# Attention and expert block on one core: four pieces of vector work and three pieces of matmul work stand at other places of the sequence loop

## The reference

```python
q, k, v = (einsum(layernorm(x), W) for W in (Wq, Wk, Wv))       # 16 heads of 64
sim = 50 * tanh((q @ k.T) / 8 / 50)                             # causal mask behind it
x = x + softmax(sim) @ v @ Wo.T
t = layernorm(x)
shared = gelu(t @ sw1 + sb1) @ sw2 + sb2
probs = softmax(t @ gate_w + gate_b); top 2 of 8 experts per token
y_e = gelu(t @ w1[e] + b1[e]) @ w2[e] + b2[e]
x = x + sum of the two chosen probs[e] * y_e + shared
```

## Time and profile before

| What | Value |
|---|---|
| median of 3 runs | 2253.5 us (2251.34 to 2255.41) |
| the profiled execution's own time | 2243.76 us |
| its span | 2242.0 us |
| TensorE busy | 1976.0 us, 88% |
| VectorE busy | 1557.3 us, 69% |
| ScalarE busy | 1420.5 us, 63% |
| GpSimd busy | 1021.2 us, 46% |
| mean granted TensorE clock | 0.955 of full speed |

### The profile page before, as it was taken

One profiled execution on the slowest core, in us unless ns is written; L12 is line 12 of the kernel. 1 busy time (PEld: TensorE's weight loads), 2 busy tenths in 40 slices (PEclk: granted clock), 3 DMA queues, 4 the chain that ended last, 5 costly groups with the idle time before them and its releaser, 6 DMA issues.

```text
span 2242.0 us, 39929 instructions
## 1 busy us (share of the span) xinstructions
PE 1976.0 (88%) x14653; PEld 1542.8 (69%) x14653; DVE 1557.3 (69%) x2803; ACT 1420.5 (63%) x2170; POOL 1021.2 (46%) x1195
## 2 busy tenths in 40 slices
PE   6799898989898988898989899898998975699898
PEld 4577666666666666666667667666666653699898
DVE  4578686767777776767677776777677686566565
ACT  6678576757676757676766766676666652344444
POOL 3445354544454444454535353445354551544344
PEclk9999999999999999999999999999999987799999
DMA  3000000100000000000101010101010102765564
GB/s 122 1 10 20 20 29 20 30 20 20 29 20 29 20 29 20 15 34 12 37 10 39 10 39 10 38 10 39 10 39 1 39 25 98 217 190 172 158 186 142
DMA packets 73665, 112.51 MB, mean 50 GB/s; under 512 B 9715, under 2 KB 52218, under 8 KB 73476
## 3 DMA queue, kind: packets, MB, share of 16 engines
q1 hardware_dynamic: 58468, 67.86, 10.7%
q0 software_dynamic: 15008, 42.10, 5.0%
HBM read 63.10 MB, written 48.65 MB: 50 GB/s over the span
## 4 chain that ended last, share of the span: by engine, by line
PE 53%; DVE 34%; ACT 9%; issue 3%; DMA 1%; POOL 0%; DVEq 0%; SPq 0%; POOLq 0%
PE bank_o L1238 8%; DVE norm L796 6%; PE ring L1196 6%; PE ring L1217 4%; DVE q_lo L785 4%; DVE kT L780 4%; PE ring L1144 3%; PE ring L1222 3%; PE ring L1150 3%; PE ring L1145 3%; PE ring L1203 3%; ACT prob L591 3%; ACT prob L585 2%; DVE oTl L810 2%; DVE oTh L808 2%
## 5 line engine op out<-in xcount | busy, mean ns | idle before, releaser
L508 POOL TENSOR_SCALAR_AFFINE_SELECT prob<-prob 128x256 f32<-128x256 f32 x512 | 221.3, 454 | 692.4 <-ACT prob L591 692.3
L585 ACT ACTIVATE prob<-ring 128x1024 f32<-128x1024 f32 (+1 forms) x384 | 328.2, 877 | 257.6 <-PE ring L1222 254.0
L780 DVE TENSOR_TENSOR kT<-ring,kT 64x512 fp32r<-64x512 f32 x256 | 176.3, 689 | 319.7 <-ACT kT L598 315.2
L1238 PE MATMUL bank_o<-prob,v 128*32 128x512 f32 (+3 forms) x4096 | 328.2, 464 | 77.0 <-DVE weighed L801 66.3
L520 POOL TENSOR_TENSOR key_sum<-prob 128x768 f32<-128x768 f32 x128 | 245.5, 1918 | 248.2 <-PE bank_d L1252 236.5
L591 ACT ACTIVATE prob<-prob 128x1024 f32<-128x1024 f32 (+1 forms) x384 | 344.0, 914 | 5.2
L1238 PEld LDWEIGHTS bank_o<-prob,v 128*32 128x32 f32 x4096 | 122.6, 115 | 253.9 <-issue 168.2
L1217 PE MATMUL ring<-qT,kT 128*128 128x256 f32 (+3 forms) x1024 | 245.2, 342 | 52.3 <-DVE row L933 11.8
L1217 PEld LDWEIGHTS ring<-qT,kT 128*128 128x128 f32 x1024 | 171.2, 194 | 131.4 <-issue 67.7
L796 DVE RECIPROCAL norm<-bank_d 128x512 f32<-128x512 f32 x64 | 214.9, 3357 | 46.1 <-PE bank_d L1252 44.3
L1222 PE MATMUL ring<-q_lo,kT 128*128 128x256 f32 (+3 forms) x1024 | 231.9, 328 | 0.0
(11 more groups left out here) (224 smaller groups left out, 4742.4 us busy)
## 6 DMA issues: line engine op xcount, KB each, us to landing
xin<-first SPq DMA_DIRECT2D x71, 257.0 KB, 3.1
xin<-second SPq DMA_DIRECT2D x71, 129.0 KB, 2.4
xin<-base SPq DMA_DIRECT2D x71, 128.0 KB, 2.4
x_next<-in_x SPq DMA_DIRECT2D x16, 512.0 KB, 4.8
x_res<-in_x SPq DMA_DIRECT2D x16, 512.0 KB, 4.3
raw_e<-in_w SPq DMA_DIRECT2D x4, 1024.0 KB, 6.7
first<-pad SPq DMA_DIRECT2D x9, 257.0 KB, 4.7
second<-pad SPq DMA_DIRECT2D x9, 129.0 KB, 7.4
```

What stands on the lines that cost most here:

```text
L508: last = nc.gpsimd.affine_select(out=diag, in_=diag, compare_op=ALU.is_ge, fill=0.0, base=0, pattern=[[0, 2], [1, P]], channel_multiplier=-1)
L585: nc.scalar.activation(probs[p % PROBS][u][:, :, :], slot[:, :, 0:UNIT_COLS[u]], ACT.Tanh, scale=SCALE / SOFTCLAMP).then_inc(act_emptied, 1)
L780: last = nc.vector.tensor_tensor(kT[head_rows[1 - h], h, :], slot[r, 1, :], kT[r, h, :].bitcast(F32), ALU.subtract)
L1238: last = pe.matmul(bank_o[h * QD:(h + 1) * QD, j * P:N], v[:, j, f:f + QD], probs[(2 * quad + h // 2) % PROBS][u][:, h % 2, at:at + N - j ...
```

## The change

The change moves code and removes or adds no arithmetic. For TensorE: in pair 4 `project_out(i, 0)` stands behind `project_qk`; the last two pieces of the projection of sequence `i - 1`, 6 and 7, both stand in pair 2, one right behind the scores and one behind `project_v`, so pair 3 has none; in pair 5 `hidden` stands behind `values`, in front of `turn_logits`. For VectorE: `place_tokens` stands in front of `empty_qk` in pair 0; `choose` has gone from pair 7 to pair 6, in front of `empty_qk`; `split_values(i - 1, 7)` stands in front of `empty_qk` in pair 2, and `add_attention` at the end of pair 2 where it stood in pair 3; `layernorm_guess` and `layernorm_newton` stand in front of `empty_qk` in pair 3. For ScalarE: `exp_gate` stands two tanh and one exp earlier in pair 6.

```diff
@@ ScalarE, pair loop @@
                     clamp(i, p, 2)
                     exponentiate(i, p, 2)
+                    if i >= 1 and p == 6:
+                        exp_gate(i - 1)
                     clamp(i, p, 0)
                     clamp(i, p, 1)
                     exponentiate(i, p, 0)
-                    if i >= 1 and p == 6:
-                        exp_gate(i - 1)
                     if p >= 3:
                         exponentiate(i, p, 1)
...
@@ VectorE, pair loop @@
                     if chunk is not None:
                         weigh_values(*chunk)
+                    if p == 0 and i >= 2:
+                        place_tokens(i - 2)
                     if p == 1 and i >= 1:
                         split_values(*chunk)
+                    if p == 2 and i >= 1:
+                        split_values(i - 1, PAIRS - 1)
                     if p == 3 and i >= 1:
-                        add_attention(i - 1)
+                        layernorm_guess(2, i - 1)
+                        layernorm_newton(2, i - 1)
                     if p == 6 and i >= 1:
                         split_hidden(i - 1)
+                        choose(i - 1)
                     if p + 1 < PAIRS:
                         empty_qk(i, p + 1)
...
                     if p == 7 and i >= 1:
-                        choose(i - 1)
                         add_shared(i - 1)
                     if chunk is not None and p != 1:
                         split_values(*chunk)
-                    if i >= 2 and p == 0:
-                        place_tokens(i - 2)
...
                     if p == 2 and i >= 1:
-                        split_values(i - 1, PAIRS - 1)
+                        add_attention(i - 1)
...
                     if p == 3 and i >= 1:
-                        layernorm_guess(2, i - 1)
-                        layernorm_newton(2, i - 1)
                         normalise_rows(i - 1)
...
@@ TensorE, pair loop @@
-            MIDDLE = {4: (turn2,), 5: (gate, hidden), 7: (shared_out,)}
-            LATE = {5: turn_logits, 7: count_earlier}
+            MIDDLE = {4: turn2, 5: gate, 7: shared_out}
+            LATE = {5: (hidden, turn_logits), 7: (count_earlier,)}
...
-                    if p >= 4:
+                    if p > 4:
                         project_out(i, p - 4)
-                    elif i >= 1 and p != 2:
+                    elif i >= 1 and p < 3:
                         project_out(i - 1, p + 4)
                     if p + 1 < PAIRS:
                         project_qk(i, p + 1)
                     elif i + 1 < NSEQ:
                         project_qk(i + 1, 0)
+                    if p == 4:
+                        project_out(i, 0)
...
                     if p == 2 and i >= 1:
-                        project_out(i - 1, PAIRS - 2)
+                        project_out(i - 1, PAIRS - 1)
                     if p >= 2:
                         values(i, p - 2)
```

More of the change, by code:

```diff
@@ L1343, in _ @@
                         project_qk(i + 1, 0)
+                    if p == 4:
+                        project_out(i, 0)
                     if i >= 1 and p in MIDDLE:
-                        for piece in MIDDLE[p]:
-                            piece(i - 1)
+                        MIDDLE[p](i - 1)
                     if i + 1 < NSEQ and p == 6:
@@ L1368, in _ @@
                     if i >= 1 and p in LATE:
-                        LATE[p](i - 1)
+                        for piece in LATE[p]:
+                            piece(i - 1)
             i = NSEQ - 1
```

## The result

The changed kernel takes 2080.5 us (median of 4 runs, 2080.15 to 2084.75), the kernel before 2253.5 beside it (2251.34 to 2255.41). The ratio is 0.9237, with a 95% interval of 0.9221 to 0.9253. The forecast was 2122 and its range began at 2104: the sign was right, and the gain is 173 us where 131 were forecast. The profiled execution took 2080.42 us, with a span of 2078.6.

The account below looks back on a forecast made before the run. TensorE's queue with its VectorE waits sets the time. Pairs sum to 104.6 us, plus 1.5 low clock 106.1: 122 gained over 13 sequences, 10 beside them; 2243.8 becomes 2112, plus 9.7 is 2122. Range 2104 to 2186, likeliest case 2106 to 2148.

Parts of the forecast that it names:

- Some low clock will stay ... I allow 1.5: Per sequence, 1.5 us allowed for low clock at the new gaps of pairs 3 and 5, against 4.6 before.
- Clocks below 1.00 stand in two pairs alone: In the one sequence read by pairs, only pair 1 (0.93) and pair 4 (0.89), those with the longest waits.
- The pairs: New times of pairs 0 to 7 in one sequence, 104.6 us together against 114.17, before the low clock allowance.
- The median of the runs is 9.7 us above it: Whole kernel: 9.7 us added to the forecast profiled execution of 2112 to give 2122.
- First and last sequences: The sequence before the 13 and the one behind them were given 10 us of gain together.
- Shared port: The layer norm moved to pair 3 would run beside GpSimd's scatters, not its sum of keys, and take 2.3 us.
- the layer norm met the sum of keys: Rival, chance 0.10: in pair 3, 3.4 us more in front of the keys' low part, 48 us, 2170.
- So there is room of 4: Pair 4: normalised rows end near 3.5 us into the pair, TensorE asks 7.4 into it.
- Hidden and gelu: Pair 5: with `hidden` behind the values, 1.0 of 1.34 us comes back as a wait on ScalarE; pair takes 15.0.
- come back at the new gaps: Rival, chance 0.10: low clock returns at the gaps of pairs 3 and 5 and costs 43 us, 2165.
- only change their name: Rival, chance 0.05: ScalarE would pace every pair as it does pair 3; no change, 2250.
- the scatter held VectorE: Rival, chance 0.04, slower: `normalise_rows` waits for a scatter's landing; decides at some 14 us, at 16 gives 2275.

Follow-up runs that it names:

- gap_1_6: The changed kernel with 4 reciprocals on VectorE ahead of the weighing in pair 1, which made a TensorE wait of 1.83 us; 2107.5 us.
- ln_back: The changed kernel with the layer norm of pair 3 back behind the low parts of keys and queries, next to the normalisation; 2120.3 us.
- hidden_only: The kernel before with one edit, `hidden` behind the values of pair 5; 2246.8 us, ratio 0.999.
- hidden_back: The changed kernel with `hidden` in front of the values of pair 5 again; 2079.3 us.
- gap_2_5: The changed kernel with 5 reciprocals on VectorE ahead of the weighing in pair 1, which made a TensorE wait of 2.82 us; 2136.0 us.
- attention_only: The kernel before with only the moves of the residual, the layer norm, `split_values` and the pieces of the output projection; 2210.4 us.

## Why the prediction fell short

The mechanism was right: TensorE's queue with the VectorE waits in it set the time, and the waits went as named. The size was off by 41.5 us, in these terms.

- **"Some low clock will stay ... I allow 1.5".** This is the step that failed. Measured is none in 13 sequences, which is 19.5 us. `gap_1_6` shows that even a gap of 1.83 us leaves the clock at 1.00 when it stands by itself. The earlier trace rows has 1.34 with a clock of 1.00, and this was in the text and was not followed. It was thin evidence, though: the clocks were read in one sequence. "Clocks below 1.00 stand in two pairs alone" holds for that one and not for the stage, where the low clock also stands behind `hidden` in 8 of 13 sequences and behind the three short waits at the turn of the sequence in 5.
- **The pairs.** 104.6 forecast, 103.80 measured, 10.4 us over 13. Pair 2 (15.9 against 15.61) and pair 3 (9.65 against 9.42) carry two thirds of it. The new wait in pair 3 was put at 1.4 and is 1.1.
- **"The median of the runs is 9.7 us above it".** I carried the distance of one profiled execution of the old kernel over to the new one. The new kernel's profiled execution is at its median. The kernel before scattered from 2241.0 to 2259.2 in 27 runs, the changed one within 4.6 us in 4. In the 27 runs time and granted clock move against each other (correlation -0.69), which points to the low clock as the source of the scatter; this is argued and not shown. The term is 9.7 us.
- **First and last sequences.** 10 forecast, 10.9 measured: the part behind the 13 sequences takes 496.0 us instead of 509.8, and the part ahead of them 2.9 more. The four terms make 19.5 + 10.4 + 9.7 + 0.9, or 40.5 of 41.5; the last us is rounding in the forecast's steps.
- **The range.** Its lower ends, 2106 and 2104, don't follow from their terms. With the low clock at nothing (19.5) and half a us of error per sequence (6.5), 2122 becomes 2096. The measured 2080.5 lies below that too.
- **Shared port.** That L738 would take 0.18 beside a scatter held (0.17), in 13 sequences. In sequence 1 there are no scatters yet, and the rival came true there: the layer norm met the sum of keys.

```profile
176.64 1.75 DVE L752 TENSOR_TENSOR newton<-newton,minus_half 128x4 f32<-128x4 f32 x1
```

```profile
176.55 1.83 POOL L520 TENSOR_TENSOR key_sum<-prob 128x768 f32<-128x768 f32 x1
```

```profile
PE ring L1218 <- DVE kT L780: 2.0, 1, 2.0
...
PE ring L1223 <- DVE q_lo L785: 0.9, 1, 0.9
```

The two waits are 2.9 us, and behind them the clock goes low (0.72 on average from 180 to 186 us), which costs 1.7 more. Other waits of sequence 1 go: 1.3 on `q_lo` and two of 0.8, against a new 1.0 on gelu. That makes 2.7 of the 2.9 us by which the 13 sequences start later. `ln_back` shows what the same meeting costs in every sequence.

The forecast also left out that the other layer norm, that of the next sequence in pair 1, changes its partner. The reciprocal no longer holds it back, so it now meets the sum of keys that it had missed.

```profile
1085.97 1.25 DVE L738 TENSOR_SCALAR var_eps<-mean_var 128x4 f32<-128x4 f32 x1
```

This took 0.18 in the earlier trace rows, and the stretch up to the normalisation takes 4.85 us (1085.97 to 1090.82) instead of 2.28. It costs no time, since TensorE transposes these rows only in pair 6.

- **"So there is room of 4".** Wrong, without harm. I counted 1.38 for the normalisation; it waited 0.26 for the last scatter and then took 4.46 beside the sum of keys. It ends at 1019.19, and `turn2` starts at 1020.10: 0.9 was left. I had looked up the layer norm's partner on GpSimd, and not that of the normalisation.
- **Hidden and gelu.** 1.0 of new wait and 15.0 for the pair, as forecast. The forecast's own terms were 0.3 gained in pair 5 and 0.65 lost in pair 6, but it did not say that the move is then worth nothing, which `hidden_only` and `hidden_back` show.
- **The rivals.** The low clock did not come back at the new gaps; the waits did not only change their name, but for that of `hidden`; the scatter held VectorE for 0.26 us, far from 14.

## What to carry to other kernels

Where the clock is below 1.00 behind a wait, count the wait and the low clock behind it together. Do it over many iterations and not one, since the low clock stood behind other waits from sequence to sequence, and count short waits that stand close together as well. Taking out one of several waits hands part of the low clock to the others; here it came back in full once no wait above 1.1 us was left. Before small VectorE work is moved, look up what GpSimd does beside it at the new place, in the first iteration too, and beside each instruction that follows. A move that trades a wait on one engine for one on another should be costed as a difference: here it was 1.33 against 1.02, and no time.

## What the runs showed of the hardware

- The same gap of 2.82 us brought the low clock in 8 of 14 sequences, 4.79 in all, 1.83 in none. In `gap_2_5` low and 1.00 alternated from the second sequence on.
- Three waits of 0.83, 0.84 and 0.60 us, the last of which ended 2.6 us behind the first, had the low clock behind them in 5 of 13 sequences of the kernel before, in 10 of `hidden_only` and in none of `attention_only`.
- Four operations of 128 x 256 numbers took 4.46 us beside GpSimd's sum of keys and 1.38 in the layer norm of the earlier trace rows; fourteen small ones took 2.62 instead of 5.9. The Trainium skill (SBUF — State Buffer, the section on who interferes with whom) has the shared ports as an exclusive lock for a whole instruction. The trace agrees as far as it goes: the single small operations that took over 1 us instead of 0.17 lie beside a tensor-tensor operation of GpSimd and end within 0.04 us of its end (in `ln_back` 1030.94 and 1030.91, 1032.33 and 1032.30), and beside its scatters L738 took 0.17.
